# Two stagings of a sequence, a first quantisation moved forward, and earlier first projections in a four-stage transformer kernel

## The reference

```python
x = L0_attn_x                                                      # 8 x 512 x 128, float32
x = x + _L0_attn_ref(_layernorm(x, axis=-1), ...)                  # attention 0
x = x + _L0_ffn_ref(_layernorm(x, axis=-1), w_gate, w_up, w_down)  # FFN 0
x = x + _L1_attn_ref(_layernorm(x, axis=-1), Wq, Wk, Wv, Wout)     # attention 1
x = x + _L1_ffn_ref(_layernorm(x, axis=-1), ...)                   # FFN 1 (experts)

def _L0_attn_ref(x, ...):            # H, D = 16, 64; feature map elu(t) + 1
    KV = jnp.einsum('bshd,bshd->bhd', K, v);  Ksum = jnp.sum(K, axis=1)
    Z = 1.0 / (Q * Ksum[:, None, :, :] + EPS)
    out = jnp.einsum('bshd,hdo->bso', Q * KV[:, None, :, :] * Z, wo) + bo
    return jax.nn.gelu(out)

def fp4_linear(x, w):                # FFN 0: blocks of 16 rounded to a grid, then dequantised
    return jnp.einsum('bsk,nk->bsn', fp4_quant_dequant(x), fp4_quant_dequant(w))
```

## Time and profile before

| | |
|---|---|
| Median of 3 runs | 973.84 us (972.89 to 976.39) |
| The profiled execution | 973.46 us |
| Its span in the profile | 971.6 us |
| Busy: PE, DVE, ACT, POOL | 875.3, 735.6, 522.2, 455.7 us |
| Attention 0 ends | 246.1 us from the span's start |
| FFN 0 ends | 397.5 us |

### The profile page before, as it was taken

One profiled execution on the slowest core, in us unless ns is written; L12 is line 12 of the kernel. 1 busy time (PEld: TensorE's weight loads), 2 busy tenths in 40 slices (PEclk: granted clock), 3 DMA queues, 4 the chain that ended last, 5 costly groups with the idle time before them and its releaser, 6 DMA issues. The chain is left out here.

```text
span 971.6 us, 18284 instructions
## 1 busy us (share of the span) xinstructions
PE 875.3 (90%) x6457; PEld 580.4 (60%) x6457; DVE 735.6 (76%) x1499; ACT 522.2 (54%) x772; POOL 455.7 (47%) x601
## 2 busy tenths in 40 slices
PE   5799999997778777579999999998889999999998
PEld 4677777774556555334454445453557667766775
DVE  5888898868799995588889888988676555646542
ACT  4577777887344545437777777777622223222220
POOL 4133322314556666325566566455554454355344
PEclk9899999998999999759999999999999999999999
DMA  9200000000000002753445454300000000000000
GB/s 289 62 12 12 11 11 11 1 11 0 5 1 12 1 12 65 164 123 90 93 114 111 89 125 94 86 9 14 12 0 22 1 22 22 11 11 22 11 11 11
DMA packets 35638, 43.33 MB, mean 45 GB/s; under 512 B 4826, under 2 KB 27770, under 8 KB 35570
## 3 DMA queue, kind: packets, MB, share of 16 engines
q1 hardware_dynamic: 35569, 42.43, 17.8%
HBM read 21.21 MB, written 15.07 MB: 37 GB/s over the span
## 5 line engine op out<-in xcount | busy, mean ns | idle before, releaser
L1707 ACT ACTIVATE PT<-PS 128x1024 f32<-128x1024 f32 x160 | 162.8, 1023 | 60.5 <-PE PS L1491 60.2
L1761 POOL TENSOR_SCALAR_AFFINE_SELECT PT<-PT 128x256 f32<-128x256 f32 (+1 forms) x224 | 96.9, 448 | 118.5 <-ACT PT L1707 116.7
L2173 POOL TENSOR_TENSOR PRE_sb<-PRE_sb,VA 128x512 f32<-128x512 f32 x64 | 82.3, 1285 | 132.4 <-DVE PRE_sb L2241 132.3
L2139 ACT ACTIVATE sg_d<-PS 128x512 f32<-128x512 f32 x64 | 38.2, 597 | 159.9 <-PE PS L1231 159.9
L2241 DVE TENSOR_TENSOR PRE_sb<-sg_d,PS 128x512 f32<-128x512 f32 x64 | 43.9, 688 | 85.3 <-ACT sg_d L2139 84.7
L426 ACT ACTIVATE E<-PS,m 128x512 f32<-128x512 f32 x128 | 85.5, 688 | 27.8 <-PE PS L314 19.0
L1476 PE MATMUL PS<-kS,qS 48*128 48x384 bf16 (+3 forms) x512 | 75.0, 317 | 17.4 <-DVE spread L1934 9.7
L1506 PE MATMUL PS<-PT,VA 128*32 128x512 f32 (+3 forms) x1024 | 89.5, 445 | 0.7 <-POOL PT L1761 0.7
L1798 DVE TENSOR_REDUCE negm<-PS 128x2 f32<-128x1024 f32 x64 | 77.9, 1222 | 15.8 <-PE PS L1480 14.7
L471 POOL TENSOR_SCALAR Qs<-Qs 128x1024 f32<-128x1024 f32 x32 | 34.2, 1069 | 106.7 <-ACT Qs L407 106.7
L1801 DVE TENSOR_REDUCE negm<-PS 128x2 f32<-128x768 f32 x64 | 61.2, 956 | 9.9 <-PE PS L1480 8.6
(11 more groups left out here) (312 smaller groups left out, 2249.0 us busy)
## 6 DMA issues: line engine op xcount, KB each, us to landing
qk_rows<-parts SPq DMA_DIRECT2D x32, 192.0 KB, 2.8
qS<-qk_rows SPq DMA_DIRECT2D x32, 192.0 KB, 4.1
kS<-qk_rows SPq DMA_DIRECT2D x32, 192.0 KB, 4.4
xs_sb<-XN_sb SPq DMA_DIRECT2D x23, 256.0 KB, 2.3
qk_rows<-parts SPq DMA_DIRECT2D x32, 128.0 KB, 2.8
X_sb<-in_x_dram SPq DMA_DIRECT2D x8, 256.0 KB, 6.6
qk_rows<-parts SPq DMA_DIRECT2D x32, 64.0 KB, 2.5
out_dram<-X_sb SPq DMA_DIRECT2D x8, 256.0 KB, 2.3
```

What stands on the lines that cost most here:

```text
L1707: nc.scalar.activation(PT[:, quad % 2, u, :], PS[:, b:b + 2, :].rearrange("p b n -> p (b n)"), ACT.Exp).then_inc(exp_ready, 1)
L1761: nc.gpsimd.affine_select(out=v, in_=v, pattern=[[0, 4 if u == 4 else 2], [1, P]], compare_op=ALU.is_ge, fill=0.0, base=0, channel_multipl ...
L2173: nc.gpsimd.tensor_tensor(acts[:, s, f, :], acts[:, s, f, :], W[:, slot, s, :], ALU.mult).then_inc(weighted, 1)
```

## The change

It does the following. In attention 0, sequence 1 has a load semaphore of its own and is normalised in chunk 9 of turn 0 (statistics at chunk 2) and not chunk 14. There are two staging buffers (`xs_even`, `xs`), and a staging waits for `g_ready` of one sequence less. The output is cut into four and four chunks around `turn_x`, not six and two. In turn 7 `sum_att`, its statistics and `norm_x(0)` come earlier, and the first sequence's quantisation is spread over chunks 9 to 13; `ks` of sequence 7 is copied one chunk before the turn's end. Sequence 1 is quantised half in attention 0 and half at the start of FFN 0. In FFN 0 the projections of sequence 0 and of sequence 1's query come one turn sooner; in the last turn VectorE quantises the second half before the statistics. The last normalisation and the last parts of sequence 1 go into attention 1's block.

```diff
             def stage(i, slot):
                 wait_apart(sp, g.turns_s, normed, i + 1)
                 if not is_seq(i, 1):
-                    sp.wait_ge(g_ready, i)
-                sp.dma_start(xs[:, :, :], XN[:, bass.ds(i * NT, NT), :]).then_inc(staged, 16)
+                    sp.wait_ge(g_ready, i - 1)
+                sp.dma_start(x_slots[slot][:, :, :], XN[:, bass.ds(i * NT, NT), :]).then_inc(staged, 16)
...
                 if not is_seq(i, 0):
-                    output(i - 1, 1 - slot, range(0, 6))
+                    output(i - 1, 1 - slot, range(0, 4))
                 if not is_seq(i, LAST):
-                    turn_x(i + 1)
+                    turn_x(i + 1, 1 - slot)
                 if not is_seq(i, 0):
-                    output(i - 1, 1 - slot, range(6, NC0))
+                    output(i - 1, 1 - slot, range(4, NC0))
...
+                    if u == 2 and is_seq(i, 0):
+                        dve.wait_ge(x1_loaded, 16)
+                        stats(1)
+                    elif u == 4 and is_seq(i, LAST):
+                        stats_att(0)
+                    elif u == 7 and is_seq(i, LAST):
+                        norm_x(0)
...
+                    if u == 9 and is_seq(i, 0):
+                        normalised(1)
+                    elif u == 14 and is_seq(i, 0):
+                        dve.wait_ge(x_loaded, 16 * (NB - 2))
+                    elif u == 9 and not is_seq(i, LAST):
                         stats(i + 1)
...
+                    elif u == 14 and not is_seq(i, LAST):
                         normalised(i + 1)
+                    elif u == 14 and is_seq(i, LAST):
+                        stats_att(1)
+                    elif u == 15 and is_seq(i, LAST):
+                        keep_ks(LAST)
+                    if is_seq(i, LAST) and u in X0_UNITS:
+                        quantise_x0(X0_UNITS.index(u))
+                if is_seq(i, 0):
+                    keep_x_low(1)
...
             norm = Steps(dve, final_steps)
+            quantise_second_x()
             for i in range(NB):
                 make_h(i, 0)
-                if i < LAST:
+                if 0 < i < LAST:
                     quantise_x(i + 1)
                 quantise_h(i, 0)
                 make_h(i, 1)
+                if i == LAST:
+                    quantise_h(i, 1)
...
-                quantise_h(i, 1)
+                if i < LAST:
+                    quantise_h(i, 1)
```

More of the change, by code:

```diff
@@ L270, in _ @@
             sp.dma_start(WO[:], w["wo0"]).then_inc(o_loaded, 16)
-            for b in range(1, NB):
+            load_x(1, x1_loaded)
+            for b in range(2, NB):
                 load_x(b, x_loaded)
@@ L510, in _ @@
                 ratio(LAST, LAST % 2, c)
-            pool.wait_ge(g.factor_ready, NB + 1)
-            factor(NB + 1)
         @block.vector
@@ L592, in norm_x, with quantise_x0 @@
                 dve.sem_inc(g.xn_ready, 1)
+            x0 = g.xq[:, :, :].rearrange("p t (b k) -> p (t b) k", k=QB)
+            x0_chain = Steps(dve, x0_steps)
+            def quantise_x0(part):
+                y, pw, mg = (blocks(t) for t in (q_x0.y, q_x0.pw, q_x0.mg))
+                ch = x0_chain
+                if part == 0:
+                    dve.wait_ge(g.xn_ready, 1)
+                    ch.step(nc.vector.tensor_reduce(q_x0.am, x0, AX.X, ALU.max, apply_absolute_value=True))
+                elif part == 1:
+                    ch.wait()
+                    ch.link(nc.vector.tensor_scalar(q_x0.sc, q_x0.am, 1.0 / 6.0, 1e-12, ALU.mult, ALU.max))
+                    ch.step(nc.vector.reciprocal(q_x0.inv, q_x0.sc))
+                elif part == 2:
+                    ch.wait()
+                    ch.step(nc.vector.scalar_tensor_tensor(out=y, in0=x0, scalar=TIE_DOWN, in1=q_x0.inv.unsqueeze(2).broadcast_to(list(y.shape)),
+                                                           op0=ALU.mult, op1=ALU.mult))
+                elif part == 3:
+                    ch.wait()
+                    ch.step(nc.vector.tensor_scalar(pw.bitcast(I32), y.bitcast(I32), 0x7F800000, None, ALU.bitwise_and))
+                else:
+                    ch.wait()
+                    ch.step(nc.vector.tensor_scalar(mg, pw, 1.0, MAGIC, ALU.max, ALU.mult))
             def keep_output(i):
@@ L1784, in period @@
                         pr.third_part(pool, i + 2, 1)
-            for m in range(2):
-                pr.first_rest(pool, 2, m)
-            for m in range(2):
-                pr.third_part(pool, 2, m)
+            factor_and_shift(nc, g, pool, NB, 2 * NB, 1, 2)
+            for n in (1, 2):
+                if n > 1:
+                    for m in range(2):
+                        pr.first_rest(pool, n, m)
+                for m in range(2):
+                    pr.third_part(pool, n, m)
             in_periods(pool, period)
```

301 lines of the change are left out of this document (178 added, 123 removed).

## The result

The changed kernel takes 969.41 us (median of 6 runs, 968.02 to 970.90) beside 974.88 (6 runs of the kernel before, 972.89 to 976.39). The ratio is 0.9946, its 95% interval 0.9930 to 0.9962: 5 us faster, and forecast were 14. The profiled execution took 968.88, its span is 966.9; before they were 973.46 and 971.6, so 4.6 and 4.7 less. The prediction said 960, and 969.4 lies outside its range of 952 to 967.

A forecast was written before the change was run, and what follows sets the result against it. Bound by TensorE in attention 0 and from slice 19, by VectorE in FFN 0. Terms -3.0 + 6.0 - 6.0 - 2.8 - 8.0 = -13.8 from 973.46 gave 959.7, with 0.4 for the median 960; range 952 to 967.

The forecast's parts named there:

- Part A: Attention 0, start of sequence 1: normalised at chunk 9, its keys' product begins sooner, -3.0 us, bounds 1.5 and 3.4.
- Part B: Attention 0, ends of turns 1 to 5: output in four and four makes TensorE wait for staging, +6.0 us.
- Part C: End of attention 0: quantisation moved into turn 7 lets the last output start sooner, -6.0 us, bounds 3 and 6.5.
- At the full clock 3.43 + 0.43 (transposes) + 3.60: End of attention 0: length of the last output from 231.5 at full clock, bringing its end to 239.0.
- clock low at 231.5: End of attention 0: the lower bound, 3 us gained, if the clock is low when the last output starts.
- Part D: Start of FFN 0: sequence 1's quantisation partly moved to attention 0, the rest in a VectorE wait, -2.8 us.
- so I subtract 0.8: Start of FFN 0: 0.8 us taken off the 3.60 gain for three steps running beside GpSimd's clearing of VA.
- Part E: End of FFN 0: second half quantised before the statistics, last normalisation and parts moved out, -8.0 us, bounds 6 and 9.4.
- 0.8 to 1.6 back: FFN 0, turns 6 and 7: us lost as first_rest and third_part of sequence 0 run beside VectorE's bit steps.
- Part F: Start of attention 1: work moved behind the barrier delays sequence 1's rows by about 2.4 us, within room: 0, bounds 0 and +2.
- What is gained ahead of it should stay gained: From slice 19 on: the change moves nothing on TensorE's path there, so earlier gains remain.
- the clock falls at each stall: Rival, attention 0's turns: each staging wait lowers the clock, costing about 3.2 us more, six times; 979 us, 6 in 100.

The follow-up runs named there:

- run 1: The changed kernel with a turn's output cut into six and two chunks again, both staging buffers kept: 961.60 us, ratio 0.9853.
- run 2: The kernel before with only the output cut into four and four chunks, one staging buffer: 978.92 us, ratio 1.0036.
- run 4: The changed kernel with, in turns 1 to 6, the next sequence's statistics at chunk 4 and normalisation at chunk 11: 958.32 us, ratio 0.9824.
- run 10: The changed kernel with run 4's sooner statistics and normalisation, but one staging buffer: 958.07 us, ratio 0.9812.
- run 11: The changed kernel with the five VectorE steps of the first sequence's quantisation moved back behind turn 7: 973.05 us, ratio 0.9966.
- run 7: The changed kernel with nine additional unread matmuls of 128x512 ahead of attention 0's last output: 965.73 us, ratio 0.9900.
- run 3: The changed kernel with GpSimd's clearing of ones and VA moved behind its first rescaling of x in FFN 0: 964.85 us, ratio 0.9890.
- run 5: The changed kernel with VA cleared by ScalarE and not GpSimd, which sets only the ones: 967.32 us, ratio 0.9907.
- run 12: The changed kernel with GpSimd's first_rest of sequence 0 done on 16 of its 512 columns: 964.90 us, ratio 0.9879.
- run 9: The changed kernel with the edits of run 4, run 5, run 6 and run 7 together: 952.09 us, ratio 0.9742.
- run 6: The changed kernel with eight additional unread matmuls of 128x512 in each of TensorE's two waits at FFN 1's start: 966.58 us, ratio 0.9908.
- run 8: The changed kernel with GpSimd's factor of the second sequence, in turn 7, behind sequence 6's last ratio: 969.34 us, ratio 0.9932.

## Why the prediction was wrong

- **Part A was right** (-3.2 for -3.0), in the path and the clock. Two of its steps were off and met by luck: the transposes came at 32.38 and not 33.6, but the low half of x then waited for VectorE's own query steps and began at 35.04, so that the key sums followed when the prediction had them.
- **Part B was right in cause, and in size with some luck.** 2.9 + 3.2 = 6.1 us against 6.0. Runs 1, 2, 4 and 10 show the whole of it: the staging waits for the normalisation, the buffer is beside the point, and the cut turns that into a wait of 1.3 us and a turn 1.0 longer. The forecast had 1.2 in each of five turns; it was 1.0 in four and 2.1 in turn 2, where TensorE waited 2.28. There the normalisation (line 116, at 84.40) took 1.83 us for 1.10 in the other turns, with a GpSimd ratio beside it at 85.09.
- **Part C was mis-sized, -3.6 for -6.0.** That the moved steps cost next to nothing inside turn 7 is shown by run 11. The failed step is the term 3.43 in "At the full clock 3.43 + 0.43 (transposes) + 3.60". A wait of 2.71 was left ahead of the output, the granted clock behind it was 0.50, and it was 4.95 us from the start of the four chunks to the transposes behind them. Run 7 fills the wait and has 3.67 for 5.11. The lower bound of 3 had named it ("clock low at 231.5"), and I chose the other end. The remaining 0.9 is that the output began at 235.43 and not 234.5 (231.5, and 3 from A and B): `weigh` began 0.4 later than that sum has it, and the ratio "that I put at 1.0" took 1.48 beside VectorE's rescaling.
- **Part D failed, -0.7 for -2.8.** The failed step was "the excess, 0.8, comes where GpSimd computes at the same time", and with it "so I subtract 0.8". The row's 1.34 us came beside single GpSimd instructions; here a run of clearings stood, and line 164 waited 3.8 us, till nearly all were done. Before, the same clearings (246.08 to 250.09) ran while VectorE waited for the first `hh`, and that `hh` (0.89) and the reduce behind it (0.69) took no longer beside them. The change put a step into that gap that did not run beside them. Runs 3 and 5 show it, by moving the clearing in time and to another engine. The Trainium skill (SBUF — State Buffer, Who interferes with whom) says that a VectorE instruction in a two-port mode and a GpSimd instruction block each other, whoever comes first for its whole length. By that rule the trace agrees in kind; I had weighed it as one clearing per step, and the step waited for more than one clearing of 1.8.
- **Part E was mis-sized, -6.7 for -8.0.** The statistics did leave the path. The term "0.8 to 1.6 back" measured 2.6 (1.8 in turn 6; in turn 7 it was 1.6, of which 0.8 had been there before): 9.2 - 2.6 = 6.6. Run 12 shows turn 6's share; turn 7's is read from the rows alone.
- **Part F was right in the end, and wrong on the way.** The first scores came 28.2 us behind the barrier, 1.3 late and past the 28 that the prediction had named as a sign of being wrong. The failed step is that only the rows' delay was counted: the `first_rest` and `third_part` of the next sequence now ran beside VectorE's two casts of the row maxima, which took 1.5 us more (404.75 and 407.04), the same effect as in D and E. No run was made for this, but in run 9 GpSimd began that pair at 392.41, behind the casts; they took 0.18 each, and the first scores came 25.0 behind the barrier. By 433 us all but 0.3 of it was back.
- **"What is gained ahead of it should stay gained" was wrong by 2.7 us.** In FFN 1 the changed kernel's clock fell at the dearer of two stalls (run 6), while the profiled execution of before had the cheaper case: which of the two a profile has is luck as far as these runs show.
- Of the rivals, "the clock falls at each stall" was too simple in both directions. Behind the staging waits of 1.3 us at the ends of turns 3 to 5 the next turn stays at 27.4 us in all nine profiles that have them; behind the one of 2.3 us the clock fell in two of the eight profiles that have it (runs 3 and 5). The Trainium skill (TensorE: Matmul & The Clock Gate, What's actually happening) calls the chip's monitor of TensorE's activity free-running, and says for the warm-up at a kernel's start that the number of slow matmuls varies from run to run. By that rule outcomes as different as those of the table below are no surprise, and the profiles agree, though each is of another kernel.

Sum of the misses: 2.4 in C, 2.1 in D, 1.3 in E, 2.7 in FFN 1, 0.6 in small ones: 9.1, from -13.8 to -4.7.

## What to carry to other kernels

Ask of a wait which of its conditions comes last before adding a resource for another one: the second buffer was worth nothing, a normalisation three chunks sooner 9 us. Before moving a step of VectorE into a gap, read what GpSimd does there, and count all its instructions in a row, not one. Where TensorE is left with a stall of 2 us or more ahead of work on the path, price that work at both clocks, in every stage behind the change as well. Spare matmuls that fill such a wait cost nothing here, and took away the dear case: 2.7 us in FFN 1, and 1.4 ahead of the last output. Compare the profiles stage by stage before putting down a gain to an edit: in runs 4 and 11 a difference of 2.7 us came from FFN 1, which neither touches.

## What the runs showed of the hardware that was not expected

The same stall brings TensorE's clock to the lower level in one profile and not in another, or sooner in one and later in another. Two places, from the profiles (the wait ahead is 2.71 us at the output in all but the first, sixth and seventh column; FFN 1 is from the first stalled matmul to the first with `asum`):

| | before | after | 1 | 3 | 4 | 7 (output filled) | 11 | 12 |
|---|---|---|---|---|---|---|---|---|
| Last output, first four chunks | 6.69 | 5.11 | 3.67 | 6.70 | 5.37 | 3.67 | 6.56 | 5.10 |
| FFN 1's stretch | 13.4 | 16.1 | 16.2 | 16.1 | 13.4 | 13.4 | 13.4 | 15.0 |

The other profiles lie between these: 5.08 to 5.37 at the output in runs 5, 6, 8 and 10, 6.02 in run 2; in FFN 1 15.0 in run 2, 16.1 in runs 5 and 8, 13.4 in run 10. With the same instructions at these places that is a spread of 3 us at either, as large as the effects that were to be measured. Every profile is of another kernel, so whether one kernel's executions differ as much is not shown; the kernel with both places filled (run 9) has 951.1 in its profiled execution and a range of 3.2 us over its runs, so something else still varies.

VectorE's bit step waited out several GpSimd clearings in a row: 3.8 us behind three of them here, 1.8 in run 3 behind the rest of one and the whole of the next. It didn't come in between two of them.
